# Scores of four heads at once, maxima by pairs of heads, in a fused decoder layer

## The reference, cut to what matters

```python
scores = einsum('bhqd,bhkd->bhqk', q, k) / sqrt(32)
attn = softmax(scores, axis=-1)                     # over the keys
std = einsum('bhqk,bhkd->bhqd', attn, v)
w = einsum('bhqn,hn,bhkn->bhqk', qa, amplitudes, ka)   # splat: qa, ka from q, k
w = w / (sum(w, axis=-1) + 1e-8)
dgsa = einsum('bhqk,bhkd->bhqd', w, v)
x = layernorm(x + ((1 - blend) * std + blend * dgsa) @ Wo)
x = layernorm(x + scan(ctx) * silu(x))              # state = state * dA + dBu, 16 states
x = layernorm(x + ffn(x))                           # ternary gate, up and down weights
```

## Time and profile before

| what | value |
|---|---|
| median of the timed runs | 1519.27 us |
| profiled execution | 1525.26 us, of it the span 1523.5 us |
| mean granted clock | 0.868 |
| busy PE / DVE / ACT / POOL | 1288.5 / 1172.2 / 753.9 / 162.7 us |
| share of the chain that ended last, PE / DVE / ACT | 48% / 24% / 7% |
| four attention loops together | 550.7 us, PE busy 492.2 |

### The profile page before, as it was taken

The page is one execution under the profiler, slowest core; times in us unless marked ns, Lnnn a source line. Parts: engine busy times, 40 slices in busy tenths (PEclk is TensorE's granted clock), DMA queues, the critical chain, the costliest instruction groups (busy, mean ns, idle before and its releaser), DMA issues.

```text
span 1523.5 us, 15252 instructions
## 1 busy us (share of the span) xinstructions
PE 1288.5 (85%) x5466; PEld 556.9 (37%) x5466; DVE 1172.2 (77%) x1233; ACT 753.9 (49%) x1086; POOL 162.7 (11%) x211
## 2 busy tenths in 40 slices
PE   4673857979689999999899998999899998897896
PEld 3342312323245542223355432323354432223453
DVE  5877997977989997658789997656889997686323
ACT  6765434535466644335476644424477544442231
POOL 0000111100111121000101210000101210001001
PEclk9765988989789998689899997957799997989898
DMA  6854753434339862304159663222169662231131
GB/s 190 274 170 126 144 125 82 90 82 107 91 102 259 198 156 52 69 17 108 50 144 259 170 154 65 58 69 42 51 155 260 170 137 59 56 90 28 63 97 55
DMA packets 88987, 178.16 MB, mean 117 GB/s; under 512 B 11424, under 2 KB 22176, under 8 KB 88912
## 3 DMA queue, kind: packets, MB, share of 16 engines
q1 hardware_dynamic: 69664, 109.29, 24.0%
q0 software_dynamic: 18432, 67.12, 22.8%
q10 hardware_dynamic: 816, 0.79, 0.2%
HBM read 97.21 MB, written 12.85 MB: 72 GB/s over the span
## 4 chain that ended last, share of the span: by engine, by line
PE 48%; DVE 24%; ACT 7%; issue 7%; DMA 4%; POOL 1%; SPq 0%; DVEq 0%; POOLq 0%; ACTq 0%
PE ps L1413 8%; DVE ST L818 8%; PE ps L1214 8%; PE ps L1230 7%; PE ps L1201 4%; PE ps L1373 4%; DVE MX L873 4%; DVE ST L810 4%; PE ps L1357 3%; ACT PT L649 3%; DMA GU<-gu_tiles 2%; DMA WP<-proj_tiles 2%; PE ps L1292 2%; PE ps L1218 2%; PE ps L1170 2%
## 5 line engine op out<-in xcount | busy, mean ns | idle before, releaser
L818 DVE TENSOR_TENSOR_SCAN ST<-dA,ST 128x1024 f32<-128x1024 f32 x128 | 294.1, 2298 | 8.5 <-ACT dA L529 5.7
L649 ACT ACTIVATE PT<-ps 128x1024 f32<-128x1024 f32 x128 | 130.8, 1022 | 236.0 <-PE ps L1218 235.8
L1413 PE MATMUL ps<-V,GU 128*128 128x512 f16 x1024 | 239.3, 389 | 7.4 <-DVE V L1004 5.6
L445 POOL DMA_DIRECT2D YA<-ST x128 | 109.3, 854 | 1094.3 <-DVE ST L821 1030.3
L873 DVE TENSOR_REDUCE MX<-ps 128x4 f32<-128x2048 f32 x64 | 146.5, 2290 | 97.6 <-PE ps L1201 97.6
L529 ACT ACTIVATE dA<-DL,Aneg 128x511 f32<-128x511 f32 x256 | 169.3, 712 | 99.9 <-DVE ST L818 99.5
L1214 PE MATMUL ps<-QK 32*128 32x512 f32 x512 | 165.8, 727 | 35.9 <-ACT PT L649 32.5
L821 DVE TENSOR_TENSOR ST<-ST,BC 128x1024 f32<-128x1024 f32 x128 | 159.9, 1249 | 4.4
L810 DVE TENSOR_TENSOR ST<-DU,BC 128x1024 f32<-128x1024 f32 x128 | 155.8, 1218 | 0.0
L1373 PE MATMUL ps<-WP,HL 128*128 128x512 f32 x512 | 143.5, 424 | 9.8 <-DMA WP<-proj_tiles 9.4
L1413 PEld LDWEIGHTS ps<-V,GU 128*128 128x128 bf16 x1024 | 97.3, 100 | 144.5 <-issue 31.5
(11 more groups left out here) (230 smaller groups left out, 1560.6 us busy)
## 6 DMA issues: line engine op xcount, KB each, us to landing
YA<-ST POOLq DMA_DIRECT2D x128, 512.0 KB, 7.1
BC<-bc_rows SPq DMA_DIRECT2D x64, 512.0 KB, 5.4
GU<-gu_tiles SPq DMA_DIRECT2D x64, 256.0 KB, 8.1
WP<-proj_tiles SPq DMA_DIRECT2D x64, 256.0 KB, 7.2
ST<-in_L_ffn_w_gate_up_dram SPq DMA_DIRECT2D x16, 256.0 KB, 3.3
gu_tiles<-BC SPq DMA_DIRECT2D x16, 256.0 KB, 2.1
proj_tiles<-HL SPq DMA_DIRECT2D x16, 256.0 KB, 2.2
XIN<-in_x_dram SPq DMA_DIRECT2D x4, 1024.0 KB, 8.5
```

Source lines behind the costliest of these rows:

```text
L649: nc.scalar.activation(PT[:, kt % 2, 2 * p:2 * p + 2, :], ps[:, 4:6, :], ACT.Exp, scale=SCALE).then_inc(s_exp, 1)
L818: nc.vector.tensor_tensor_scan(flat, dA[:, a, :, :].rearrange("p e s -> p (e s)"), flat, 0.0, ALU.mult, ALU.add).then_inc(s_scan, 1)
L1413: last = mm(ps[:, f % F_RING, :], GU[:, t % GU_RING, k, m * P:(m + 1) * P], XHL[:, z, k, :], start=(k == 0 and z == 0), stop=(k == KT - 1 ...
```

## The change

Scores: in groups 0 to 2 `score_quad` computes all four heads of a step, on banks 2 to 5, with one signal for both of ACT's exps, which read banks 2 and 3, then 4 and 5. It waits for both exps of the step before. The last group keeps `score_pair` on banks 4 and 5.

Maxima: those of group 0 are computed as before. Those of groups 1 to 3 go by pairs of heads (`max_pair`), each pair into banks 0 and 1, and each reduced by a DVE instruction of its own (128x1024); the second pair waits for the reduction of the first. Every step computes one tile of maxima, one step further ahead than the group (`group_in`), so the last step of a group already starts the group after the next one's first tile, behind the bias row.

Scans: in groups 0 to 2, `slot_halves` spreads three or four halves over as many steps; two halves stay in steps 1 and 3. Splat: the keys are transposed in the last step of group 2, and the product with V moves into the first step of group 3, behind the denominators. DVE normalises at the start of every group, ahead of any maxima.

```diff
@@ slot_halves
-                third = max(1, len(mine) // 3)
-                return [[], mine[:third], [], mine[third:]]
+                extra = max(0, len(mine) - 3)
+                if len(mine) < 3:
+                    return [[], mine[:1], [], mine[1:]]
+                return [mine[:extra]] + [[h] for h in mine[extra:]]
@@ order of the maxima
-        GROUPS = {0: (1, 2, 3, 4, 4), 1: (0, 2, 3, 4, 4), 2: (0, 1, 3, 4, 4), 3: (0, 0, 0, 0, 0)}
+        def group_in(j, kt):
+            n = KT * (j + 1) + kt + GROUPS_AHEAD
+            return divmod(n, KT) if n < KT * NG else None
+        SCORE_BANK, MAX_BANK, TURN_BANK, KEY_BANK = 2, 0, 0, 1
@@ scalar
+                            first_bank = SCORE_BANK + 2 * p if j < NG - 1 else 4
+                            nc.scalar.activation(PT[:, kt % 2, 2 * p:2 * p + 2, :], ps[:, first_bank:first_bank + 2, :],
@@ vector, max_groups
-                    nc.vector.tensor_reduce(MX[:, g, 0:P:D], ps[:, 0:HG, :], AX_X, ALU.max).then_inc(s_mx, 1)
+                    for part in range(2):
+                        bank = MAX_BANK
+                        dve.wait_ge(s_xs, maxima_done(b, j, g, part))
+                        nc.vector.tensor_reduce(MX[:, g, 2 * D * part:2 * D * (part + 1):D], ps[:, bank:bank + 2, :],
+                                                AX_X, ALU.max).then_inc(s_mx, 1)
@@ vector, attention_phase
+                        if j > 0 and c == 0:
                             normalise(b, j - 1)
+                        if j == NG - 1 and c == 0:
                             splat_kv(b)
+                        if j < NG - 1 and group_in(j, c):
+                            jm, g = group_in(j, c)
+                            max_groups(b, jm, g, g + 1)
@@ tensor
+            def max_pair(b, j, g, part):
+                if g == 0 and part == 0:
+                    pe.wait_ge(s_br, NG * b + j)
+                pe.wait_ge(s_mx, maxima_done(b, j, g, part) - 1)
+                for h in (2 * part, 2 * part + 1):
+                    rows = slice(D * h, D * h + D)
+                    last = mm(ps[:, MAX_BANK + h % 2, :], QK[rows, 0, j, g * P:(g + 1) * P], QK[rows, 1, j, :],
+                              start=True, stop=True, tile_position=(D * h, 0))
+                last.then_inc(s_xs, 1)
+            def score_quad(b, j, kt):
+                ...
+                    pe.wait_ge(s_exp, exps_done(b, j, kt, 0) - 1)
+                ...
+                for h in range(HG):
+                    rows = slice(D * h, D * h + D)
+                    mm(ps[:, SCORE_BANK + h, :], QK[rows, 1, j, kt * P:(kt + 1) * P], QK[rows, 0, j, :],
+                       start=True, stop=False, tile_position=(D * h, 0))
+                for h in range(HG):
+                    row = slice(D * h, D * h + 1)
+                    last = mm(ps[:, SCORE_BANK + h, :], one_row[row, :], BR[row, j % 2, :],
+                              start=False, stop=True, tile_position=(D * h, 0))
+                last.then_inc(s_s, 2)
@@ tensor, attention_phase, groups 0 to 2
+                        score_quad(b, j, kt)
+                        if j == 0 and kt == 0:
+                            max_pair(b, 1, 0, 1)
+                        if kt == KT - 1:
+                            transpose_max(b, j + 1)
+                            if not group_in(j, kt):
+                                transpose_keys(b)
+                        elif kt > 0:
+                            max_pair(b, *group_in(j, kt), 0)
+                        if kt > 0:
+                            values(b, j, kt - 1, 6)
+                            if kt == KT - 1 and group_in(j, kt):
+                                max_pair(b, *group_in(j, kt), 0)
+                            values(b, j, kt - 1, 7)
+                            if kt < KT - 1:
+                                max_pair(b, *group_in(j, kt), 1)
+                        else:
+                            for part in range(2):
+                                max_pair(b, *group_in(j, kt), part)
+                    values(b, j, KT - 1, 6)
+                    if group_in(j, KT - 1):
+                        max_pair(b, *group_in(j, KT - 1), 1)
+                    values(b, j, KT - 1, 7)
```

More of the change, by code:

```diff
@@ L1325, in attention_phase @@
-                        if j == KV_GROUP and kt == 0:
-                            pe.wait_ge(s_kvm, 4 * b + 4)
-                        if hi > lo:
-                            max_scores(b, j + 1, hi - 1, hi)
-                        if j == NG - 1 and kt == 0:
-                            pe.wait_ge(s_br, NG * (b + 1))
-                            pe.wait_ge(s_kvm, 4 * b + 3)
-                            mm(ps[:, 0, :], QAK[:, 4, 0:P], QAK[:, 0, :], start=True, stop=True).then_inc(s_den, 1)
-                            if not last_batch:
-                                prep_context(b + 1)
@@ new lines, in attention_phase @@
+                    values(b, j, KT - 1, 6)
+                    if group_in(j, KT - 1):
+                        max_pair(b, *group_in(j, KT - 1), 1)
+                    values(b, j, KT - 1, 7)
+                j = NG - 1
+                for kt in range(KT):
+                    for p in range(2):
+                        pe.wait_ge(s_exp, exps_done(b, j, kt, p) - 1)
+                        if kt == 0:
+                            pe.wait_ge(s_br, NG * (b + 1))
+                        score_pair(b, j, kt, p)
+                        if kt > 0:
+                            values(b, j, kt - 1, 6 + p)
+                    if kt == 0:
+                        pe.wait_ge(s_kvm, 4 * b + 3)
+                        mm(ps[:, 0, :], QAK[:, 4, 0:P], QAK[:, 0, :], start=True, stop=True).then_inc(s_den, 1)
+                        pe.wait_ge(s_ka, b + 1)
+                        for k in range(KT):
+                            last = mm(ps[:, 1, :], QAK[:, 2, k * P:(k + 1) * P], V[:, k, :], start=(k == 0), stop=(k == KT - 1))
+                        last.then_inc(s_kv, 1)
+                        if not last_batch:
+                            prep_context(b + 1)
+                    if kt in (1, 2):
+                        if not last_batch:
@@ L1339, in attention_phase @@
                             prep_in(b + 1, 2 * kt - 2)
                             prep_in(b + 1, 2 * kt - 1)
-                        if j == NG - 1 and kt in (1, 2):
-                            pe.wait_ge(s_qr0, 2 * b + 2)
-                            for g in (2 * kt - 2, 2 * kt - 1):
-                                if g >= 2:
-                                    pe.wait_ge(s_at, NG * b + g - 1)
-                                mm(ps[:, g % 2, :], QAK[:, 3, g * P:(g + 1) * P], QAK[:, 0, :], start=True, stop=True).then_inc(s_num, 1)
@@ L1347, in attention_phase @@
-                    for bank in (6, 7):
-                        values(b, j, KT - 1, bank)
-                    if j == 0:
-                        for k in range(KT):
-                            last = nc.tensor.transpose(ps[:, 1, k * P:(k + 1) * P], QAK[:, 1, k * P:(k + 1) * P], ident[:, :])
-                        last.then_inc(s_kat, 1)
+                        pe.wait_ge(s_qr0, 2 * b + 2)
+                        pe.wait_ge(s_kvm, 4 * b + 4)
+                        for g in (2 * kt - 2, 2 * kt - 1):
+                            if g >= 2:
+                                pe.wait_ge(s_at, NG * b + g - 1)
+                            mm(ps[:, g % 2, :], QAK[:, 3, g * P:(g + 1) * P], QAK[:, 0, :], start=True, stop=True).then_inc(s_num, 1)
@@ L1355, in out_products @@
+                for bank in (6, 7):
+                    values(b, j, KT - 1, bank)
                 def out_products(r, groups_of_heads):
```

101 lines of the change are left out of this document (41 added, 60 removed).

## The result

The changed kernel takes 1609.49 us, the median of four runs (1606.31 to 1617.89); the kernel before takes 1518.37 in the runs beside it (1514.86 to 1522.54). The ratio is 1.068, 95% interval 1.060 to 1.076. The forecast was 1588 with a range of 1530 to 1640.

A forecast was written before the change was run, and what follows sets the result against it. Loops PE-bound, price set by clock: 549 us at 2.4 GHz, 735 at 1.2; 45% of time low gives 619, +68 over 551. Profiled 1525.3 becomes 1593, less 6 for the median: 1588, range 1530 to 1640.

The forecast's parts named there:

- The layout: Attention loops, PE and DVE timed side by side: second group 31.9 us instead of 24.0 at 2.4 GHz, 43.6 at 1.2.
- Rival 3: Score quad: its four K=1 bias products run one behind another, a quad takes 2.4 us, total 1617; chance 0.08.
- The balance: PE's work per loop step at 2.4 GHz: 5.63 us before, 5.0 after, so 0.6 saved.
- The sum of waits: PE's idle before pairs of maxima in all four loops: about 50 to 90 us, against 32.0 in 24 waits before.
- the 45%: Share of the attention loops' time taken to pass at 1.2 GHz, against 36% before; gives loops of 619 us, +68.
- rival 2: Attention loops: the clock stays low most of the time, 75% of it, +126 us, about 1645; chance 0.12.
- rival 1: Attention loops: not slower because the clock stays up, 1518 us, or 1495 with cheap maxima; chance 0.14.
- rival 4: Attention loops: two heads of maxima are cheap (0.46 us), clock as before, about 1549 us; chance 0.08.
- The move of the splat's key-value product: Fourth group: the product lies on PE's path, adding 4.4 us; batch 3 from 31.6 to 36, batches 1 and 2 36.1 to 40.5.
- the waits of ACT's exps for PE: Attention loops: these waits were to shrink per exp, a sign that the forecast was right.

The follow-up runs named there:

- e4: Changed kernel with DVE's first-half reduction ahead of normalise and the scan's three instructions queued singly between reductions: 1506.24 us, 1.002 of before.
- e6: e5 with the splat's affinities and weights on DVE in group 0 queued as two pieces behind the scan's pieces: 1482.36 us, 0.974 of before.
- e8: Changed kernel with scores by pairs on banks 4 and 5, maxima halves on banks 0-1 and 2-3, and e4's DVE order: 1572.91 us.
- e3: Changed kernel with the quad issued as two pairs (scores, bias, scores, bias), no wait between: 1595.62 us.
- e5: e4 with PE doing denominators before the first half of the maxima in the last step of groups 0 and 1: 1498.49 us.
- e7: Kernel before with only the change's spread of scan halves over steps, acting in batch 0 alone: 1524.48 us against 1517.57 for before.

## Why the prediction was right, and where its sizes were off

**The cause is shown.** PE's queue hangs on each half of the maxima, with the next quad behind it, and DVE's queue holds whole blocks ahead of the reductions. Moving the reduction ahead and taking the scan apart, with nothing else changed, gives back the 91 us lost (103 by the medians, ratio to before 1.002, e4); the scan in pieces is worth 87 alone, the order against normalise 18 to 27 alone. Somewhat over half of what e4 gives back in the loops is waiting, 57.1 of 101.3 us; the rest is PE's work at a higher clock. The layout had two waits of 6.2 and 3.1 us in the second group; they are 6.02 and 2.87.

**Prices on PE.** The quad was taken at 1.2 and takes 1.20, a pair of maxima at 0.95 and takes 1.05 (1314.10 to 1315.15 in e4). Rival 3, biases one behind another, is out. The balance that the prediction drew from them was 0.6 us saved per step at full clock, 5.63 to 5.0; without its waits a step of e4 is 5.21 (1317.01 to 1322.85, less 0.63), so 0.4 is saved. At 1.2 GHz the layout had 9.5 in place of 10.31, and the traced step is cheaper: 8.98 us (654.18 to 663.16).

**The sum of waits was mis-sized.** The prediction gave 50 to 90 us of idle before the maxima, beside a row of 32.0. By the same row there are now 280.8 (163.1 and 117.7); by PE's own row 117.7. Both lie above: the figure was not made from the layout, whose 9.3 us times twelve groups is already 112. As a rise of all idle time in the loops it is 73.4.

**Groups.** With the layout's values at either level and the share of time that the row's clock gives, batch 1 should take 40.7, 38.8 and 41 us in its first, second and fourth group; traced are 45.9, 40.9 and 39.5; batch 3's second group should take 35.5 and takes 35.9. The first group failed most: I had not followed the splat's block on DVE, which stands ahead of a scan and a reduction there. Taking it apart (e6) gave 16 us over four batches. In all the loops came to 631 in place of 619, which is 12 of the 21 us between 1588 and 1609. The other 9 are the step from the profile to the median: the profiled execution of before lay 6 us above its median, that of after lies 3 below.

**The clock came out right, in part by luck.** Weighted mean 0.76 with 0.77 forecast, or 47% of the loops' time at 1.2 GHz with 45. No sum led to the 45%: it was chosen between the 36% of before and the 75% of rival 2. With 36% the forecast would have been some 15 us lower, with 75% some 57 higher, so that the time hung on this choice as well as on the layout. Rival 2 (75%) and rival 1 (the clock stays up) are out, and rival 4 (1549) too. By the Trainium skill's rule on cycling PSUM banks (TensorE: Matmul & The Clock Gate, A second HAM failure mode: psum-queue depth-cycling) the clock swings between both levels; the trace agrees, falling behind 6.02 and again behind 2.87 us of wait with a return between them, and the share stayed far from rival 2's.

**Steps that were wrong.** The move of the splat's key-value product was priced at 4.4 us per batch. Batch 1's fourth group went from 36.1 to 39.5 at an equal clock (0.95 and 0.96), but batch 3's from 31.6 to 30.0 with the clock up from 0.78 to 1.00, against 36 forecast. And the waits of ACT's exps for PE did not shrink: 235.8 us in 109 waits became 279.2 in 65, fewer and twice as long, since ACT too hangs on PE's waits; in e4, with these cut down, they are 189.7 in 64.

**Open.** The move of the key-value product and the tile taken one step further ahead were not tried alone, so that what they cost in e4 and e6 isn't known. Why one wait is followed by 1.2 GHz (1.14 us) and another isn't (1.39 us at 1310.98 in e4) was not tested either; within e4 a wait of 1.39 us at 629.35 is followed by the lower level and the equal one at 1310.98 is not. And why e8, with less idle time than e4, has the lower clock is open, so that the worth of the quad at an equal clock isn't known beyond the table of steps.

## What to carry to other kernels

When a buffer is cut in two so that two engines must alternate on it, read the consumer's queue between the two uses: every instruction there can now stand on the path, whatever its engine's busy share. Put the consumer's reduction first and cut the long blocks behind it into single instructions (here 4.7, 3.4 and 2.0 us; for a wait of 0.9 us it brought nothing). A change can hold a real gain, here the quad, which at 1.2 GHz takes 2.0 us off a step against e8, under a loss in an order that costs no more than a few lines to mend. And part of what a wait costs can stand elsewhere, in work done at a lower clock: 44 of the 101 us in e4.

## What the runs showed that I had not expected

- How the eight products of a quad are sorted does not matter: 1.20 us as scores and then biases, 1.20 as pair, bias, pair, bias (e3). Four tiles on row groups of their own run beside each other in both. The Trainium skill (TensorE: Matmul & The Clock Gate, Measured speedup vs the span model) has 3.07 times for four such tiles; here four heads of maxima last 0.97 us and two last 1.05 (e4), so the second two are free; no run has one head alone, so the factor itself can't be compared. In e8 a half of heads 2 and 3 and the pair of scores of heads 0 and 1 behind it take 1.26 us together (1384.72 to 1385.98), where the pair alone took 1.18 before. That fits the table of steps, where halved maxima cost e8 nothing at full clock.
- The records of a half and the next quad begin within 10 to 20 ns of each other (1310.98 and 1310.99 in e4), and yet both together take 2.2 us, the sum of the two. Such starts show no gain by themselves.
- The clock does not follow idle time alone. e8, with pairs of scores, has 64.0 us idle and a clock of 0.77; e5, with quads, has 83.1 us idle and 0.87. e7's loop of batch 0 has less idle time than before and a lower clock.
- The unchanged kernel spreads over 1492.57 to 1542.57 us on one chip (13 runs) and e4 on the same chip over 1496.49 to 1512.53 (10 runs). A difference under 1% needs many runs of a kernel that spreads like that.
